# Transposed scores issued ahead of new scores inside each slot, on TensorE

## The chip, the cores and the metric

The kernel runs on one core of a Trainium2 chip. The metric is the device time of one execution in microseconds (us). Lower is better.

## The reference

Eight sequences of 512 tokens with 128 channels go through two layers.

- Layer 0: LayerNorm, then latent attention (16 heads of 8 channels, rotary embedding, causal mask) and, from the same normalised input, a mixture of 8 experts (128 to 512 to 128, ReLU, the two best gates of a softmax). Both are added to the input.
- Layer 1: LayerNorm, then attention with 16 heads of 8 whose scores are multiplied by a sigmoid gate, mixed 0.3 to 0.7 with a second attention of 4 heads of 32, mixed again 0.85 to 0.15 with a third of 4 heads of 32 that reads the mix, and an output projection; beside it a feed-forward net (128 to 512, SiLU gate, two 512 to 512 layers with exact GELU, back to 128). Both are added to the input.

Each attention is softmax(q k^T * scale) v over 512 keys. The GELU layers are evaluated once per sequence each.

## The kernel before

**Units.** All attention work is cut into groups: per sequence four of kind `a0` (layer 0, 4 heads of 8 each), four of kind `a1` (layer 1), one `ca` and one `mc` (4 heads of 32 each). A group has 8 units. Unit j works on query (or key) block c = j // 2 of 128 rows and on two heads, those of pair j % 2. So there are 80 groups and 640 units.

**Slots.** The program is one long list of slots, numbered G. Every engine walks the same list and issues in each slot what is due there. `UNIT[G]` is the unit whose scores are made in slot G, `TRANS[G]` the unit whose transposed scores are made there; it is the unit of slot G - 15 (`LAG`). A sequence takes 80 slots; in the steady part the score units fill them without a gap, in the order `a0` x4 (slots 0 to 31 of the 80), `ca` (32 to 39), `a1` x3 (40 to 63), `mc` (64 to 71), `a1` (72 to 79). In the text "slot 52" means slot 52 of a sequence's 80. Only the last sequence is laid out differently.

**What a unit does.** `score` issues two matmuls, scores of 128 queries against the keys, into banks 0 and 1. Before each it waits until VectorE has taken the row maximum of the tile that was in that bank (`pe.wait_ge(sem("max"), tile - 1)`). `reduce_unit` on VectorE (L714, and L710 with the causal mask for `a0`) takes that maximum of each. Ten slots later the maxima of a group are transposed (`max_rows`), written out by VectorE (`mrow`, L721) and sent by DMA into an extra row of the queries. 15 slots later `trans` issues the two transposed matmuls (keys against queries, with the maximum already subtracted) into banks 2 and 3; before each it waits until ScalarE has taken the exponential of the tile that was there (`sem("exp")`). `exp_unit` on ScalarE (L981) makes the probabilities. Every second slot `value` multiplies them with the values into bank 4 (8 matmuls, or 4 and 4 that sum the probabilities).

**Shapes on TensorE.** Units of `a0` and `a1` use 32 rows of the array for one head: pair 0 uses rows 0 to 63, pair 1 rows 64 to 127. In the profile their scores are `banks<-kp,qs` (32*128) and their transposed scores `banks<-qs,kp` (32*128). Units of `ca` and `mc` use 96 rows for the scores and 97 for the transposed ones, both shown as `banks<-qkc`, once as 96*128 and once as 97*128. As the lag is odd and all groups of the steady part start at even slots, score and transposed score of a slot always belong to opposite pairs there.

**The order inside a slot.** TensorE's loop is written out by hand: `score`, `trans`, `few_rows` (small projections), `value`, `few_cols` (with `max_rows`), `experts`, `ffn`, `heads`, `opening`, `between`, `mixing`, `ffn`. VectorE's is: first FFN steps, `reduce_unit`, then heads, experts, normalisations, casts (`gelu1_hi`, `gelu2_hi`, L885) and divisions. ScalarE's is: `gelu`, a copy, `exp_unit`, then experts (`hm` L1041, `h_hi` L1042), FFN, projections. All waits are semaphore counts; they name the producer's count and not a slot, so the order of TensorE's list can be altered without altering another engine's list.

**Where GELU stands.** ScalarE makes the GELU of 128x2048 at the start of slot 71 (first layer) and of slot 6 of the following 80 (second layer), with a load of its function table before (L1076) and one back for the exponential (L981).

Of the kernel before, what the change touches and what calls it, by code (L numbers as in the profile page):

```python
# [202 lines left out]
def build(nc, x_in, wide_in, lat_in, cols_in, rows_in, const_in, split_in, am_in, cons_in, b2_in, out):  # L203
# [10 lines left out]
    TRANS = {at + LAG: unit for at, unit in UNIT.items()}  # L214
# [25 lines left out]
    with ctx:  # L240
# [99 lines left out]
        def sem(name):  # L340
            if name not in sems:
                sems[name] = ctx.enter_context(nc.semaphore(name))
            return sems[name]
# [13 lines left out]
        def mm(bank, cols_, lhsT, rhs, start, stop, rows_=slice(0, P)):  # L357
            return nc.tensor.matmul(psum[rows_, bank, cols_], lhsT, rhs, start=start, stop=stop)  # L358
# [10 lines left out]
        def ch(c):  # L369
            return slice(c * P, (c + 1) * P)  # L370

        def main(g):
            return g.main >= 0

        def width(g, c):
            return (P * (c + 1), P * c) if g.kind == "a0" else (T, 0)
# [7 lines left out]
        with nc.Block() as block:  # L384

            @block.tensor
            def _(pe):
# [9 lines left out]
                def score(g, j):  # L397
                    c, pair = j // 2, j % 2
                    kw, _ = width(g, c)
                    if j == 0:  # L400
                        if main(g):
                            pe.wait_ge(sem(f"kq{g.gr}"), 32 * (g.main // NG + 1))
                        else:
                            pe.wait_ge(sem("qkc"), 96 * (g.mix + 1))
                    for s in range(2):
                        h, tile = 2 * pair + s, 2 * (8 * g.n + j) + s
                        if tile >= 2:
                            pe.wait_ge(sem("max"), tile - 1)
                        if main(g):
                            lhsT, rhs = qs[32 * h:32 * h + 32, g.gr, ch(c)], kp[32 * h:32 * h + 32, g.gr, 0:kw]  # L410
                        else:
                            lhsT, rhs = qc[0:96, h, ch(c)], kc[0:96, h, 0:kw]
                        mm(SCO + s, slice(0, kw), lhsT, rhs, True, True).then_inc(sem("score"), 1)
# [8 lines left out]
                def trans(g, j):  # L422
                    c, pair = j // 2, j % 2
                    _, q0 = width(g, c)
                    if j == 0:
                        pe.wait_ge(sem(f"qmax{g.n % 2}"), QMAX[g.n])
                    for s in range(2):
                        h, tile = 2 * pair + s, 2 * (8 * g.n + j) + s
                        if tile >= 2:
                            pe.wait_ge(sem("exp"), tile - 1)  # L430
                        if main(g):
                            lhsT, rhs = kp[32 * h:32 * h + 32, g.gr, ch(c)], qs[32 * h:32 * h + 32, g.gr, q0:T]
                        else:
                            lhsT, rhs = kc[0:97, h, ch(c)], qc[0:97, h, q0:T]
                        mm(TRA + s, slice(q0, T), lhsT, rhs, True, True).then_inc(sem("trans"), 1)
# [59 lines left out]
                def few_rows(G):  # L495
                    for k, name in enumerate(("k0", "k0r")):
                        if (b := due(G, name)) is not None:
                            taken(pe, "u", "latT", b)
                            own("n", name, b)
                            project(N, latw[:, 128 * k:128 * k + 128], latT[:, :]).then_inc(sem("n_full"), 1)  # L500
                    if (b := due(G, "v0a")) is not None:
                        own("m", "v0a", b)
                        for c in range(NC):
                            last = mm(M, slice(P * c, P * c + 96), latT[:, ch(c)], latw[:, 256:352], True, True)
                        last.then_inc(sem("m_full"), 1)
                    if (b := due(G, "v0b")) is not None:
                        own("m", "v0b", b)
                        for c in range(NC):
                            last = mm(M, slice(32 * c, 32 * c + 32), latT[:, ch(c)], latw[:, 352:384], True, True)
                        last.then_inc(sem("m_full"), 1)  # L510
                    if (b := due(G, "wo0")) is not None:
                        if b == 0:
                            pe.wait_ge(sem("b2_in"), NC * 16)
                        taken(pe, "m", "gT", b)
                        own("m", "wo0", b)
                        mm(M, slice(0, T), gT[:, :], b2[:, :], True, False)

                def few_cols(G):
                    if (u := UNIT.get(G - 10)) is not None and u[1] == 0:
                        max_rows(u[0])  # L520
                    if (b := due(G, "latT")) is not None:
                        own("u", "latT", b)
                        taken(pe, "u", "lat", b)
                        for c in range(NC):
                            last = nc.tensor.transpose(psum[0:LAT, U, ch(c)], latn[:, c, :], C("ident"))
                        last.then_inc(sem("u_full"), 1)
                    if (b := due(G, "gT")) is not None:
                        pe.wait_ge(sem("gates"), b + 1)
                        own("m", "gT", b)
                        nc.tensor.transpose(psum[0:NC * E, M, 0:P], gates[:, :, :].rearrange("p c e -> p (c e)"), C("ident")) \  # L530
                            .then_inc(sem("m_full"), 1)
# [137 lines left out]
                for G in range(FIRST_G, LAST_G):  # L669
                    if G == SETUP:  # L670
                        pe.wait_ge(sem("s_in"), 6 * 16)
                        nc.tensor.matmul(psum[:, 0, 0:1], am, cons, start=True, stop=True).then_inc(sem("s_am"), 1)
                    if G == GROUPS[0].start:
                        pe.wait_ge(sem("s_set"), 3)
                    if G in UNIT:
                        score(*UNIT[G])
                    if G in TRANS:
                        trans(*TRANS[G])
                    few_rows(G)
                    if G in VALUE_AT:  # L680
                        value(*VALUE_AT[G])
                    few_cols(G)
                    experts(G)
                    ffn(G, 0)
                    heads(G)
                    opening(G)
                    between(G)
                    mixing(G)
                    ffn(G, 1)
# [697 lines left out]
```

## Time and profile before

| what | value |
|---|---|
| median of 3 runs | 1888.39 us (1887.96 to 1888.41) |
| the profiled execution's own time | 1886.58 us |
| its span, first to last instruction | 1883.7 us |
| mean granted TensorE clock | 0.947 |
| TensorE matmul busy | 1682.3 us (89%) |
| VectorE / ScalarE / GpSimd busy | 1201.5 / 1172.5 / 691.6 us |
| DMA, share of 16 engines | 11.2% on the largest queue |

A busy row counts the time in which at least one instruction of that engine ran. PE is TensorE's matmuls, PEld its weight loads, which run beside matmuls; DVE is VectorE, ACT ScalarE, POOL GpSimd. A wait is the idle time of an engine before an instruction and the instruction whose end released it. Idle time of PEld is not idle time of PE: an earlier matmul may still run.

### The profile page before, as it was taken

What the parts mean: (1) busy time and instruction counts of PE and PEld (TensorE: products, weight loads), DVE (VectorE), ACT (ScalarE), POOL (GpSimd) and SP (SyncE); (2) the same over time, 40 slices, a digit from 0 to 9 for tenths busy, and PEclk for the clock granted to TensorE, in tenths of its full rate; (3) what the DMA queues carried; (4) which work ended last, traced back from release to release, by engine and by line L of the source; (5) the groups of instructions that cost most, each with busy time, mean ns of one, the idle gap of its engine ahead of it and who ended that gap; (6) DMA issues with size and microseconds to landing.
All of it is one profiled execution on the core that took longest, in us unless ns stands there. A gap on an engine that the chain in (4) does not pass through costs nothing.

```text
span 1883.7 us, 33377 instructions
## 1 busy us (share of the span) xinstructions
PE 1682.3 (89%) x12298; PEld 711.5 (38%) x12298; DVE 1201.5 (64%) x3100; ACT 1172.5 (62%) x2225; POOL 691.6 (37%) x672
## 2 busy tenths in 40 slices
PE   3886899889999999999999999999999999988976
PEld 1343453245323543245333543345333543222331
DVE  6545477556875587666866578566866577476623
ACT  2681765587556865687556865687657865645542
POOL 3463642255232642255322652255322631211120
PEclk9996999999999999999999999999999999978976
DMA  5101200110100101110100101110101100011010
GB/s 208 35 19 34 63 13 15 54 30 13 49 32 28 36 30 40 40 35 13 49 29 26 41 24 41 44 35 13 47 23 35 35 23 24 29 40 34 1 34 6
DMA packets 63682, 66.81 MB, mean 35 GB/s; under 512 B 8144, under 2 KB 58144, under 8 KB 62624
## 3 DMA queue, kind: packets, MB, share of 16 engines
q1 hardware_dynamic: 63520, 64.68, 11.2%
q8 instruction: 98, 1.61, 0.4%
q14 instruction: 64, 0.52, 0.1%
HBM read 40.73 MB, written 23.59 MB: 34 GB/s over the span
## 4 chain that ended last, share of the span: by engine, by line
PE 68%; DVE 15%; ACT 11%; issue 5%; POOL 1%; DMA 1%; SPq 0%; POOLq 0%; ACTq 0%; DVEq 0%
PE banks L358 66%; DVE negmax L714 7%; ACT probs L981 3%; ACT h_hi L1042 2%; ACT hm L1041 2%; DVE h L877 2%; DVE xs L814 1%; ACT L981 1%; ACT h L1076 1%; PE banks L573 1%; DVE mrow L721 1%; DVE h L872 1%; DVE r_b L902 1%; ACT L1076 1%; PE banks L580 0%
## 5 line engine op out<-in xcount | busy, mean ns | idle before, releaser
L981 ACT ACTIVATE probs<-banks 128x512 f32<-128x512 f32 (+3 forms) x1280 | 613.6, 533 | 475.4 <-PE banks L358 471.1
L714 DVE TENSOR_REDUCE negmax<-banks 128x1 f16<-128x512 f32 x768 | 492.0, 684 | 172.5 <-PE banks L358 169.1
L1141 POOL TENSOR_TENSOR h_lo<-hm,h_hi 128x512 f16<-128x512 f32 x256 | 296.7, 1160 | 387.1 <-ACT h_hi L1042 386.9
L710 DVE CUSTOM_DVE_ANT_0 scr<-banks,mask_row 128x384 f32<-128x384 f32 (+3 forms) x512 | 230.2, 487 | 211.9 <-PE banks L358 210.3
L358 PE MATMUL banks<-kp,qs 32*128 32x512 f16 (+3 forms) x1024 | 234.6, 363 | 51.5 <-DMA kp<-relk 22.5
L358 PE MATMUL banks<-probs,vp 128*32 128x512 f32 (+3 forms) x2048 | 247.3, 556 | 0.0
L1041 ACT ACTIVATE hm<-banks,cols 128x512 f32<-128x512 f32 x256 | 176.4, 689 | 113.6 <-PE banks L358 111.7
L358 PE MATMUL banks<-qs,kp 32*128 32x512 f16 (+3 forms) x1024 | 201.7, 358 | 35.2 <-ACT probs L981 33.0
L1182 POOL TENSOR_TENSOR h_lo<-h,h_hi 128x512 f16<-128x512 f32 x96 | 110.6, 1169 | 293.7 <-ACT h_hi L1070 218.3
L358 PE MATMUL banks<-w_hi,h_hi 128*128 128x128 f16 x1152 | 205.6, 221 | 0.0
L358 PE MATMUL banks<-w_lo,h_hi 128*128 128x128 f16 x1152 | 205.2, 220 | 0.0
L358 PE MATMUL banks<-w_hi,h_lo 128*128 128x128 f16 x1152 | 205.1, 220 | 0.0
L358 PE MATMUL banks<-qkc 97*128 97x512 f16 (+1 forms) x512 | 166.8, 399 | 13.8 <-DVE negmax L714 5.5
L358 PE MATMUL banks<-xh,w_hi 128*128 128x512 f16 x320 | 128.0, 400 | 54.5 <-ACT h_hi L1042 34.2
L1042 ACT ACTIVATE h_hi<-banks,cols 128x512 f16<-128x512 f32 x256 | 175.1, 684 | 0.0
L358 PEld LDWEIGHTS banks<-kp,qs 32*128 32x128 f16 x1024 | 61.1, 92 | 283.4 <-issue 108.2
L358 PEld LDWEIGHTS banks<-w_hi,h_hi 128*128 128x128 f16 x1152 | 113.4, 98 | 31.8 <-issue 12.5
L358 PE MATMUL banks<-xl,w_hi 128*128 128x512 f16 x320 | 124.9, 390 | 0.0
L358 PE MATMUL banks<-xh,w_lo 128*128 128x512 f16 x320 | 124.6, 389 | 0.0
L358 PEld LDWEIGHTS banks<-w_lo,h_hi 128*128 128x128 f16 x1152 | 113.5, 99 | 19.9 <-issue 0.8
L358 PEld LDWEIGHTS banks<-w_hi,h_lo 128*128 128x128 f16 x1152 | 113.5, 98 | 0.0
L1133 POOL TENSOR_TENSOR halves<-w,halves 128x512 f16<-128x512 f32 x64 | 74.2, 1159 | 99.4 <-ACT halves L1001 97.4
(149 smaller groups left out, 2347.7 us busy)
## 6 DMA issues: line engine op xcount, KB each, us to landing
qkc<-relm SPq DMA_DIRECT2D x96, 128.0 KB, 3.1
qs<-relq SPq DMA_DIRECT2D x64, 128.0 KB, 2.1
kp<-relk SPq DMA_DIRECT2D x64, 128.0 KB, 2.2
relm<-halves SPq DMA_DIRECT2D x32, 256.0 KB, 2.2
relq<-halves SPq DMA_DIRECT2D x16, 256.0 KB, 2.1
relk<-halves SPq DMA_DIRECT2D x16, 256.0 KB, 2.1
h<-split_in SPq DMA_DIRECT2D x3, 1024.0 KB, 5.1
xs<-x_in SPq DMA_DIRECT2D x8, 256.0 KB, 3.3
```

What stands on the lines that cost most here:

```text
L358: return nc.tensor.matmul(psum[rows_, bank, cols_], lhsT, rhs, start=start, stop=stop)
L573: last = nc.tensor.transpose(psum[:, M, ch(c)], osb[:, g.main % 2, ch(c)], C("ident"))
L710: v.tensor_tensor_reduce(scr[:, s, 0:kw], psum[:, SCO + s, 0:kw], mask_row[:, T - kw:T], -1.0, 3e38, ALU.add, ALU.min, negmax[:, g.n % 2, ...
L714: v.tensor_reduce(negmax[:, g.n % 2, c, h:h + 1], psum[:, SCO + s, 0:kw], AX.X, ALU.max, negate=True).then_inc(sem("max"), 1)
L877: v.tensor_scalar(h32[:, o, :], psum[:, U, :], V(f"hs{n}", o), None, ALU.mult) \
L981: a.activation(probs[:, c % 2, 2 * pair + s, q0:T], psum[:, TRA + s, q0:T], ACT.Exp, scale=SCALE[main(g)]).then_inc(sem("exp"), 1)
L1041: a.activation(hm[:, i % 2, :], psum[:, U, :], ACT.Relu, bias=V("b1", i))
L1042: a.activation(h_hi[:, (e + 1) % 2, hc, :], psum[:, U, :], ACT.Relu, bias=V("b1", i)) \
L1076: a.activation(h32[:, :, :], h32[:, :, :], ACT.Gelu).then_inc(sem("gelu"), 1)
L1133: p_.tensor_tensor(out=halves[:, w, 1, :], in0=w32[:, w, :], in1=halves[:, w, 0, :], op=ALU.subtract).then_inc(sem(f"low{w}"), 1)
L1141: p_.tensor_tensor(out=h_lo[:, (e + 1) % 2, hc, :], in0=hm[:, i % 2, :], in1=h_hi[:, (e + 1) % 2, hc, :], op=ALU.subtract).then_inc(sem("h ...
L1182: p_.tensor_tensor(out=h_lo[:, k % 2, o, :], in0=h32[:, o, :], in1=h_hi[:, k % 2, o, :], op=ALU.subtract).then_inc(sem("g_lo"), 1)
```

## The change

Two steps of TensorE's loop change places. Nothing else is edited: no instruction, wait, buffer or DMA is added or removed, and the lists of the other engines are the same.

```diff
                     if G == GROUPS[0].start:
                         pe.wait_ge(sem("s_set"), 3)
+                    if G in TRANS:
+                        trans(*TRANS[G])
                     if G in UNIT:
                         score(*UNIT[G])
-                    if G in TRANS:
-                        trans(*TRANS[G])
                     few_rows(G)
                     if G in VALUE_AT:
                         value(*VALUE_AT[G])
```

## Rows read from the trace of the kernel before

**Rows 1.** The page: busy time (share of the span), and the chain by engine.

```profile
PE 1682.3 (89%) x12298; PEld 711.5 (38%) x12298; DVE 1201.5 (64%) x3100; ACT 1172.5 (62%) x2225; POOL 691.6 (37%) x672
...
PE 68%; DVE 15%; ACT 11%; issue 5%; POOL 1%; DMA 1%; SPq 0%; POOLq 0%; ACTq 0%; DVEq 0%
```

**Rows 2.** Waits, whole span: engine line waited for: us in total, times, longest.

```profile
PEld banks L358 <- DVE negmax L714: 133.1, 249, 1.7
...
PEld banks L358 <- ACT probs L981: 68.8, 121, 3.6
...
PEld banks L358 <- DVE negmax L710: 42.4, 73, 3.0
```

**Rows 3.** Timeline of PE, slot 18: start us, us, instruction xcount.

```profile
832.69 0.28 PE L358 MATMUL banks<-kp,qs 32*128 32x256 f16 x2
832.70 0.34 PE L358 MATMUL banks<-qs,kp 32*128 32x384 f16 x2
```

**Rows 4.** Timeline of PE, slot 53.

```profile
919.49 0.39 PE L358 MATMUL banks<-kp,qs 32*128 32x512 f16 x2
919.81 0.61 PE L358 MATMUL banks<-qkc 97*128 97x512 f16 x2
```

**Rows 5.** Timeline of PE, slot 52 (brackets: idle before, and its releaser).

```profile
916.23 0.39 PE L358 MATMUL banks<-kp,qs 32*128 32x512 f16 x1
916.78 0.39 PE L358 MATMUL banks<-kp,qs 32*128 32x512 f16 x1 [0.17 <-DVE negmax L714]
917.10 0.61 PE L358 MATMUL banks<-qkc 97*128 97x512 f16 x2
917.63 0.64 PE L358 MATMUL banks<-probs,vc 128*32 128x512 f32 x4
```

**Rows 6.** Timeline of DVE and ACT, slots 51 and 52.

```profile
915.46 2.49 DVE L714 TENSOR_REDUCE negmax<-banks 128x1 f16<-128x512 f32 x4
915.55 1.08 ACT L981 ACTIVATE probs<-banks 128x512 f32<-128x512 f32 x2 [1.89 <-PE banks L358]
```

**Rows 7.** Timeline of PE, slot 79.

```profile
991.78 0.39 PE L358 MATMUL banks<-kp,qs 32*128 32x512 f16 x1
992.31 0.39 PE L358 MATMUL banks<-kp,qs 32*128 32x512 f16 x1
...
993.07 0.38 PE L358 MATMUL banks<-h_hi,w_hi 128*128 128x512 f16 x1
```

**Rows 8.** Timeline of PE, slot 38.

```profile
884.83 0.39 PE L358 MATMUL banks<-qkc 96*128 96x512 f16 x1 [0.21 <-DVE negmax L714]
```

**Rows 9.** Timeline of ACT, between the exponentials of slot 5 and the second GELU.

```profile
800.20 1.28 ACT L1076 ACT_TABLE_LOAD   x1
```

**Rows 10.** Timeline of PE, slots 664 to 667, first and last row.

```profile
1687.59 1.20 PE L358 MATMUL banks<-kp,qs 32*128 32x512 f16 x2 [0.59 <-DVE negmax L714]
...
1693.71 1.03 PE L358 MATMUL banks<-qkc 97*128 97x512 f16 x2
```

**Rows 11.** Timeline of PE, slots 7 and 8, behind the second GELU.

```profile
803.75 0.39 PE L358 MATMUL banks<-kp,qs 32*128 32x512 f16 x2
805.46 0.78 PE L358 MATMUL banks<-qs,kp 32*128 32x512 f16 x2 [1.33 <-ACT probs L981]
...
806.93 0.23 PE L358 MATMUL banks<-kp,qs 32*128 32x128 f16 x2
```

**Rows 12.** Timeline of DVE, slot 7.

```profile
804.17 0.69 DVE L710 CUSTOM_DVE_ANT_0 scr<-banks,mask_row 128x512 f32<-128x512 f32 x1 [0.88 <-PE banks L358]
```

**Rows 13.** Timeline of PE, slots 42 and 43.

```profile
893.99 0.71 PE L358 MATMUL banks<-qs,kp 32*128 32x384 f16 x2
...
895.84 0.39 PE L358 MATMUL banks<-kp,qs 32*128 32x512 f16 x2
```

**Rows 14.** Timeline of PE, slot 72, behind the first GELU; slot 73 starts at 977.98.

```profile
975.09 1.08 PE L358 MATMUL banks<-qs,kp 32*128 32x512 f16 x2 [2.27 <-ACT probs L981]
...
977.98 0.61 PE L358 MATMUL banks<-kp,qs 32*128 32x512 f16 x2
```

## The prediction

> **What bounds the kernel now.** I read the page first: matmuls are busy for 89% of the span, and the chain that ended last runs through TensorE for 68%, VectorE for 15% and ScalarE for 11% [rows 1]. So time is won or lost where TensorE stands still or where its list is held up. The waits over the span say by whom: the weight loads stood before maxima of VectorE for 133.1 + 42.4 = 175.5 us in 322 places, and before exponentials of ScalarE for 68.8 us in 121 [rows 2]. The first are waits of `score`, the second of `trans`. These are the two waits whose order the change swaps, and none of these sums is a gain as it stands: much of it lies beside matmuls that still run. The timelines of single slots tell what each is worth. One steady sequence repeats the last to a few hundredths, so a slot read once stands for its six or seven siblings.
>
> **Two kinds of slot.** In 48 of 80 slots both units use 32 rows a head, on opposite halves of the array. All four matmuls then run at once: scores at 832.69, transposed scores at 832.70, 0.34 us for all [rows 3]. Without a wait, either order costs the same, and with one the pair that waits still takes the other beside it. In the other 32 slots (0 to 6, 32 to 39, 47 to 54, 64 to 71, 79) one of the two fills the array, and they follow each other: transposed scores start 0.32 us behind the scores [rows 4], and two full ones take 0.44 (917.10 to 917.63 less the 0.09 of a change of tile form) [rows 5]. There the one in front can fill a wait of the other.
>
> **What the change brings, part by part.** Instructions: the same ones, 2560 score and transposed-score matmuls, no DMA moved. SP's and POOL's lists are untouched; their waits are on counts that still come.
>
> *Slot 52 and its like.* The slot's first score starts at 916.23, the second waits for its maximum until 916.78, and 0.32 and 0.53 us go by behind it before the next step at 917.63 [rows 5]. With the full transposed scores in front, they run during that wait: the exponentials they need end at 915.55 + 1.08 = 916.63 [rows 6], and 0.3 earlier once slot 51 also has its transposed scores in front. The second score then goes at about 917.04, since slot 51's scores, 0.53 later there, start their reduction at 915.69 and not 915.46 [rows 6]. The next step comes 0.31 behind, at 917.35: gain 0.3 us, seven times, 2.0 us. Slot 79 is the clean case: 0.53 us between the scores (991.78, 992.31), the next step at 993.07 [rows 7]; with the transposed scores done in the wait it comes at 992.31 + 0.32 = 992.63: gain 0.44, six times, 2.6 us. Slot 38 waits 0.21 us at its second score [rows 8]; I take 0.15, seven times, 1.0 us. In slots 34 and 48 the maxima are late because the scores before them were just in time; these move later with the swap, and I count nothing.
>
> *Ahead of the second GELU.* The table load starts as slot 5's exponentials end [rows 9], and slot 5's transposed scores come 0.3 us sooner. The GELU's input is due almost when the load ends, so I take 0.2, six times, 1.2 us. Between 0 (input later) and 0.3.
>
> *Slots 664 to 667,* in the last sequence, hold nothing but scores and full transposed scores and take 6.1 us from 1687.59 to 1693.71 [rows 10]. VectorE needs 4 x 1.25 = 5.0 us for their maxima [rows 6]: gain 1.0.
>
> Gains together: 2.0 + 2.6 + 1.0 + 1.2 + 1.0 = 7.8 us.
>
> *What is put behind a late exponential.* In slot 7 the scores go at 803.75 and the transposed scores, held by GELU and table load, at 805.46 and, 0.78 less one matmul of 0.39 later, 805.85; slot 8 starts at 806.93 [rows 11]. VectorE now uses the stall: it reduces from 804.17 (0.42 behind the score) to 805.5 [rows 12]. With the swap the scores stand behind the transposed ones and go at 805.85, their second maximum is there at 805.85 + 0.42 + 1.3 = 807.6, and slot 8's second score waits for it, 0.6 to 0.7 us after the slot's start. Queued behind it: slot 8's probabilities times values, then slots 9 and 10, each of which hands ScalarE its next tile, so little of it is absorbed. Slot 8's transposed scores are already out in front, so I take 0.56 of 0.65; five times, plus 0.3 for the first, where VectorE is late in any case: 3.1 us. VectorE's casts of the GELU's output behind these reductions move 2.1 us later too, as does GpSimd's work on them; the matmuls that read it come slots later, so I count nothing.
>
> *Slot 42* is the same in small: transposed scores at 893.99 and, 0.71 less one matmul of 0.34 later, 894.36, for exponentials that are late, and slot 43 at 895.84 [rows 3, 13]. The scores move to 894.36, their second maximum to 894.36 + 0.42 + 1.3 = 896.1, and slot 43's second score waits 0.25 to 0.3 for it: seven times, 2.1 us.
>
> *Slot 72*, behind the first GELU, has the longest stall, 2.27 us before 975.09 [rows 14], but slot 73 starts only at 977.98. The scores would go at 975.6 and their maxima be done at 975.6 + 0.42 + 1.3 = 977.3: in time. Cost 0; if the two casts behind it delayed slot 73's maxima, 0.4 each.
>
> Losses together: 5.2 us. **Sum:** -7.8 + 5.2 = -2.6, say -3 us.
>
> **Two rules of the Trainium skill.** Rows 5 show that nothing of TensorE's list passes a waiting matmul: the transposed scores, whose exponentials were ready at 916.63, start 0.32 behind the score that waited until 916.78. The Trainium skill says the same (TensorE: Matmul & The Clock Gate, Part 3: Packing small matmuls): matmuls start and end in program order. It speaks against the change: by it all 5.2 us of losses stand, whereas if scores could pass the held transposed ones the sum would be -7.8. The other rule (TensorEngine Tiling (Array Packing), Key Properties) is that a change of tiling form drains the array. The rows bear it out with 0.31 to 0.32 from one form to the next against 0.22 within one. The new order saves one change in eight value slots of a sequence (full transposed scores next to full work) and adds one in eight (full scores between 32-row and column-tiled ones): net 0; the added ones alone would be 64 x 0.09 = 5.8 us.
>
> **The rivals.**
> *B, faster: the waits for maxima are simply covered.* For it: they outweigh the waits for exponentials, 175.5 to 68.8 us [rows 2], and transposed scores in front also feed ScalarE earlier, which idles before them. Against it: most of them stand in slots where all four matmuls run at once. Slots 38, 52 and 79 wait 0.21, 0.55 and 0.53 us [rows 5, 7, 8], 1.3 a sequence; with slots 34 and 48 at half of the larger ones each it is an estimated 1.8. If all of it goes (1.8 x 7 = 12.6 us) and the losses are absorbed: 1876 us.
> *C, slower: VectorE is fed late.* Place: the slots behind a late exponential and the 32 slots of unlike shapes, where scores come 0.32 to 0.53 later. It decides from the point where the next slot starts less than 0.42 + 1.3 = 1.7 us behind the late score. Then the gains of slots 38, 52 and the GELU vanish as the maxima move along, slot 7 costs its full 0.65 and slot 72 its 0.4. Price: 6 x 0.65 + 2.1 + 8 x 0.4 = 9.2, less slot 79's 2.6: +6.6, or 1895 us. For it: VectorE idles before these reductions only because it gets them early, and slot 7 shows it clearly. Against it: most slots are over 2 us.
> *D, no effect:* the two steps are exchangeable, as rows 3 have it for 48 of 80 slots: 1888 +- 1.
>
> **How the numbers follow.** The profiled execution took 1886.58 us, 2.9 more than its span of 1883.7, and the median is another 1.8 above, 1888.39. I lay -2.7 on the median: 1885.7. Chances: forecast 0.42 (own range -6 to +1, about 1882 to 1889), B 0.27, C 0.24, D 0.07. A measurement of this kernel tells about 0.2%, 3.8 us. Faster by more: B's 0.27 and 0.12 of the forecast, 0.39. Slower by more: 0.22 of C and 0.02, 0.24. Within: 0.37. The range reaches to B's and C's prices, 1877 to 1896.
>
> **What would show it.** Right: in slots 52 and 79 the next step comes 0.3 and 0.44 us sooner; in slot 8 the second score starts about 0.6 behind the first; waits for maxima sum to less than 175.5 and those for exponentials to more than 68.8; slots of rows 3 look as before with the names exchanged. Wrong: a loss behind slot 72, a changed stretch 56 to 62 (VectorE's own pace there, where I count nothing), or four matmuls that no longer run at once.

## The result, and the profile after

The changed kernel takes 1903.59 us (median; 1903.01 to 1906.62) against 1888.40 us for the kernel before in the same comparison: ratio 1.008, 95% interval [1.0063, 1.0098], so 15.2 us slower. I had forecast 2.7 us faster, with a range to 1896: the sign was wrong and the time lies outside the range. The profiled execution took 1903.01 us, with a span of 1901.3 against 1883.7.

The page of the changed kernel, busy time and chain, as in [rows 1]:

```profile
PE 1692.0 (89%) x12298; PEld 715.1 (38%) x12298; DVE 1214.9 (64%) x3100; ACT 1170.6 (62%) x2225; POOL 694.8 (37%) x672
...
PE 69%; DVE 12%; ACT 10%; issue 5%; POOL 3%; DMA 1%; SPq 0%; POOLq 0%; ACTq 0%; DVEq 0%
```

Its waits over the span, as in [rows 2]:

```profile
PEld banks L358 <- ACT probs L981: 145.8, 236, 4.1
...
PEld banks L358 <- DVE negmax L714: 59.8, 149, 1.4
...
PEld banks L358 <- DVE negmax L710: 32.8, 52, 3.0
```

Waits for maxima fell from 175.5 to 92.6 us, waits for exponentials rose from 68.8 to 145.8. The change does to the waits what it should; their sum even falls by 6 us while the kernel gets 15 us slower. VectorE has 13.4 us more busy time for the same 3100 instructions, and POOL enters the chain with 3% instead of 1%.

TensorE in the changed kernel, slot 52, as in [rows 5] (start us, us, instruction xcount):

```profile
927.14 0.62 PE L358 MATMUL banks<-qkc 97*128 97x512 f16 x2
927.69 0.74 PE L358 MATMUL banks<-kp,qs 32*128 32x512 f16 x2
928.37 1.06 PE L358 MATMUL banks<-probs,vc 128*32 128x512 f32 x8
```

The next step comes 1.23 us behind the slot's start; it was 1.40. And slot 79, as in [rows 7]:

```profile
788.12 0.60 PE L358 MATMUL banks<-qkc 97*128 97x512 f16 x2
788.66 0.39 PE L358 MATMUL banks<-kp,qs 32*128 32x512 f16 x2
788.98 0.39 PE L358 MATMUL banks<-h_hi,w_hi 128*128 128x512 f16 x1
```

0.86 us to the next step, before 1.29: a gain of 0.43 for the 0.44 predicted. So the gains are there. Three places show how the losses arise; all three are steps that VectorE does late.

**Behind the second GELU.** TensorE in the changed kernel, slots 8 to 10, as in [rows 11]; slot 8 starts at 814.72:

```profile
815.46 0.22 PE L358 MATMUL banks<-kp,qs 32*128 32x128 f16 x1 [0.23 <-DVE negmax L710]
...
818.14 0.43 PE L358 MATMUL banks<-kp,qs 32*128 32x128 f16 x2 [0.28 <-DVE negmax L710]
...
819.86 1.93 PE L358 MATMUL banks<-probs,vp 128*32 128x512 f32 x8
```

and the same last step in the kernel before:

```profile
811.19 1.06 PE L358 MATMUL banks<-probs,vp 128*32 128x512 f32 x8
```

Slot 8's second score comes 0.74 us behind the slot's start (I had 0.6 to 0.7). What I had not: the scores of slots 9 and 10 wait for maxima as well, so that from slot 8's start to that last step 5.14 us go by and not 4.26. Then the eight matmuls take 1.93 us and not 1.06: the granted clock is 0.52 from 819.80 to 823.00, close to the lower of its two levels (1.2 of 2.4 GHz). That fall is not the swap's alone; in two other sequences the kernel before has one in these slots too (see the first experiment). Why slots 9 and 10 wait is seen on VectorE. The kernel before:

```profile
805.89 1.08 DVE L885 CAST h_hi<-h 128x512 f16<-128x512 f32 x3
807.20 0.29 DVE L710 CUSTOM_DVE_ANT_0 scr<-banks,mask_row 128x128 f32<-128x128 f32 x1 [0.22 <-PE banks L358]
```

The changed kernel:

```profile
815.82 2.06 DVE L885 CAST h_hi<-h 128x512 f16<-128x512 f32 x3
817.79 0.28 DVE L710 CUSTOM_DVE_ANT_0 scr<-banks,mask_row 128x128 f32<-128x128 f32 x1
```

and beside it, on GpSimd of the changed kernel:

```profile
816.16 1.43 POOL L1141 TENSOR_TENSOR h_lo<-hm,h_hi 128x512 f16<-128x512 f32 x1 [21.13 <-ACT h_hi L1042]
```

The casts stand behind slot 7's late maxima and in front of slot 8's. Pushed back, they meet a GpSimd subtraction that before started at 808.38, when they were over; the third of them takes 1.39 us where each took 0.42 before.

**Slot 687**, behind the first GELU of the last sequence. The kernel before, TensorE and then VectorE:

```profile
1754.69 1.09 PE L358 MATMUL banks<-qs,kp 32*128 32x512 f16 x2 [2.53 <-ACT probs L981]
1755.71 2.08 PE L358 MATMUL banks<-wide,ctxT 128*128 128x128 f32 x8
```

```profile
1752.20 1.29 DVE L714 TENSOR_REDUCE negmax<-banks 128x1 f16<-128x512 f32 x2 [0.49 <-PE banks L358]
...
1753.68 0.29 DVE L828 TENSOR_TENSOR onorm<-banks,rden 128x128 f32<-128x128 f32 x1
```

The changed kernel, TensorE and then VectorE:

```profile
1766.97 0.87 PE L358 MATMUL banks<-qs,kp 32*128 32x512 f16 x2 [2.63 <-ACT probs L981]
1767.47 0.60 PE L358 MATMUL banks<-kp,qs 32*128 32x512 f16 x2
1769.75 1.65 PE L358 MATMUL banks<-wide,ctxT 128*128 128x128 f32 x6 [1.69 <-DVE onorm L828]
```

```profile
1767.92 1.29 DVE L714 TENSOR_REDUCE negmax<-banks 128x1 f16<-128x512 f32 x2 [3.71 <-PE banks L358]
...
1769.41 0.29 DVE L828 TENSOR_TENSOR onorm<-banks,rden 128x128 f32<-128x128 f32 x1
```

TensorE stands 1.69 us for a division whose inputs were long there. It stood on VectorE's list behind maxima of scores that now sit on TensorE's list behind exponentials. So a wait of TensorE on ScalarE holds up VectorE's unrelated work, and that comes back to TensorE.

**Slot 34,** one of the slots that my prediction counted as nothing, shows the same without any late exponential. A step of TensorE waits there for the one in which VectorE writes `vc`, behind slot 33's maxima; slot 33's scores come later with the swap, as it is a slot of unlike shapes. The kernel before, then the changed kernel:

```profile
874.77 0.38 PE L358 MATMUL banks<-ident,negmax 128*4 128x128 f16 x4 [0.20 <-DVE vc L852]
```

```profile
885.54 0.38 PE L358 MATMUL banks<-ident,negmax 128*4 128x128 f16 x4 [0.46 <-DVE vc L852]
```

### The profile page after: what moved, and what is told of

It is laid out like the page before. It is cut to its first block, busy times and chain, and to the rows that moved or that the text cites. A ratio compares the mean times of both kernels' runs of the same rounds, so it can differ in the third digit from the quotient of the medians.

```text
span 1901.3 us, 33377 instructions
## 1 busy us (share of the span) xinstructions
PE 1692.0 (89%) x12298; PEld 715.1 (38%) x12298; DVE 1214.9 (64%) x3100; ACT 1170.6 (62%) x2225; POOL 694.8 (37%) x672
## 4 chain that ended last, share of the span: by engine, by line
PE 69%; DVE 12%; ACT 10%; issue 5%; POOL 3%; DMA 1%; SPq 0%; POOLq 0%; ACTq 0%; DVEq 0%
PE banks L358 67%; DVE negmax L714 5%; ACT probs L981 3%; ACT h_hi L1042 2%; ACT hm L1041 2%; POOL h_lo L1141 1%; DVE xs L814 1%; PE banks L573 1%; ACT L981 1%; DVE h L877 1%; DVE r_b L902 1%; ACT h L1076 1%; DVE h L872 1%; POOL xs L1186 0%; DVE mrow L721 0%
## 5 line engine op out<-in xcount | busy, mean ns | idle before, releaser
L358 PE MATMUL banks<-kp,qs 32*128 32x512 f16 (+3 forms) x1024 | 227.5, 366 | 41.6 <-DMA kp<-relk 22.3
L358 PE MATMUL banks<-qs,kp 32*128 32x512 f16 (+3 forms) x1024 | 210.4, 359 | 49.6 <-ACT probs L981 44.8
L358 PE MATMUL banks<-probs,vp 128*32 128x512 f32 (+3 forms) x2048 | 252.2, 566 | 0.0
L358 PEld LDWEIGHTS banks<-qs,kp 32*128 32x128 f16 x1024 | 55.2, 91 | 249.7 <-ACT probs L981 117.1
```

## The experiments

Theories, as the expectations name them: **L**, lateness: a score put behind a late exponential gives VectorE its maxima late, and its work and the next slots are late with it. **Q**, the part of L that is VectorE's queue: steps that need nothing of the late score wait behind its maxima. **K**, clock: more of the stretches fall to the lower granted clock. **V**, the diffuse part of L: VectorE gets its scores 0.3 to 0.5 us later in every slot of unlike shapes. (One expectation calls the clock theory C.) Each time stands beside that of the kernel before in the same comparison, and a difference "by ratio" is the ratio times that time. Most kernels differ in one condition alone, written here as the slots in which the transposed scores go first:

```diff
+ ahead = G in TRANS and (CONDITION)
+ if ahead:
+     trans(*TRANS[G])
  if G in UNIT:
      score(*UNIT[G])
- if G in TRANS:
+ if G in TRANS and not ahead:
      trans(*TRANS[G])
```

**Where the loss is.** Behind the second GELU:

```diff
+ CONDITION: 80 <= G < 640 and 7 <= G % 80 <= 11
```

> The swapped order only in slots 7 to 11 of each steady sequence (behind the second GELU), the old order in all others. Theory L (the loss is local: scores put behind late exponentials, there and in the first and last sequence): the trace of the full swap is longer than before by 6.6 us in total in slots 6 to 12 of these sequences, so about +6.5 us over the kernel before. Theory V (diffuse: VectorE gets its scores 0.3 to 0.5 us later in the 32 unlike slots of every sequence): at most +1.5 us.

Measured: 1894.40 against 1888.33 us, ratio 1.0019 [1.0004, 1.0033]. Single executions lie in two groups, 1884.6 to 1889.6 and 1892.7 to 1896.9, so a size can't be read from it to better than +0.8 to +6 us. The traces are sharper. Slots 6 to 11 of one sequence, in the kernel before at the full clock, in the kernel before where the clock falls, and with the swap at the full clock (window, length, busy time of each engine, granted clock, DMA share, GB/s):

```profile
1226.80:1243.00 16.20, 13.54 (x110) 5.05 (x109) 11.46 (x39) 14.66 (x22) 6.79 (x6) 1.00 0.01 2
```

```profile
1012.90:1030.70 17.80, 15.06 (x106) 5.14 (x105) 11.46 (x39) 14.74 (x22) 6.78 (x6) 0.90 0.00 1
```

```profile
1226.50:1243.60 17.10, 13.74 (x107) 5.22 (x107) 12.54 (x39) 14.70 (x22) 7.40 (x6) 1.00 0.01 2
```

From slot start to slot start that is 16.21, 17.85 and 17.10 us: 0.9 us a sequence for the swap, and 1.6 us for a fall of the clock without the swap (1.0 to 1.6 with it). It falls in two of five such sequences in the trace of the kernel before, in four in that of the changed kernel, and in one in this run's, whose profiled execution (1884.62 us) is of the lower group. That the number of such falls makes the two groups is not shown.

The first sequence alone:

```diff
+ CONDITION: G < 80
```

> The swapped order only in the first sequence (slots 17 to 79 from the start of the list), the old order from slot 80 on. Theory L: the full swap's trace has gained 4.2 us by slot 80, from slots 24 to 31, where VectorE is late with the weight splits and TensorE then shows a granted clock of 0.5; so +4 us, and it stays to the end. Theory V: the unlike slots are hardly there in this stretch, so about 0.

Measured: 1889.11 us, 1.0006 [0.9998, 1.0015]: nothing that can be told from no change; the 4 us that L expected are not there.

The last sequence alone:

```diff
+ CONDITION: G >= 640
```

> The swapped order only in the last sequence, from slot 640. Theory L: +4 us (the full swap's trace loses 6.6 us in slots 685 to 695, behind the last GELU, and gives back 3.6 in slots 662 to 673 and 706 to 710). Theory V: +2 us, spread over the stretch.

Measured: 1897.79 us, 1.0049 [1.0037, 1.0061], +9.3 us by ratio: a large part of the whole, from 38 of the 584 slots that hold both steps, and twice what L expected.

The slots of unlike shapes, in the steady sequences:

```diff
+ CONDITION: 80 <= G < 640 and (G % 80 < 7 or 32 <= G % 80 < 40 or 47 <= G % 80 < 55 or 64 <= G % 80 < 72 or G % 80 == 79)
```

> The swapped order only in the 32 unlike slots of each steady sequence (0 to 6, 32 to 39, 47 to 54, 64 to 71, 79), the old one elsewhere. Theory L: -2 to 0 us, since the gains of slots 52 and 79 are here and no late exponential is. Theory V: +5 to +9 us, most of the loss.

Measured: 1891.36 us, 1.0007 [0.9991, 1.0022]: nothing that can be told from no change, and under the +5 of theory V.

The slots in which all four matmuls run at once, without those behind the second GELU:

```diff
+ CONDITION: 80 <= G < 640 and (12 <= G % 80 < 32 or 40 <= G % 80 < 47 or 55 <= G % 80 < 64 or 72 <= G % 80 < 79)
```

> The swapped order only in the like slots of each steady sequence except 7 to 11 (12 to 31, 40 to 46, 55 to 63, 72 to 78). Theory L: the only late exponentials here are those of slots 42 and 72; the full swap's trace has 0.37 us more per sequence around slot 42 and 0.2 to 0.7 around slot 72, so +3 to +6 us. Theory C (the granted clock: what the swap costs is mostly more time at 0.5 behind longer idle stretches): no sum from single slots, a spread of runs of 5 us and more.

Measured: 1902.59 against 1888.00 us, 1.0079 [1.0066, 1.0092], +14.9 us by ratio. This was the surprise: slots in which "either order costs the same" make as much loss as the whole change. No trace shows it in full: the profiled execution took 1895.32 us, the other four 1902.36 to 1903.42, and its swapped stretches are 0.74 us a sequence longer at the same clock, some 5 us together. Its granted clock falls in slots 6 to 11 of four sequences, and those slots have the old order here.

The slots that my prediction had as gains, alone:

```diff
+ CONDITION: 80 <= G < 640 and G % 80 in (5, 38, 52, 79) or 664 <= G <= 667
```

> The swapped order only where the prediction counted gains: slots 5, 38, 52 and 79 of each steady sequence and slots 664 to 667. If those terms were right: -7.8 us. By the full swap's trace, which is 0.54 us shorter a sequence around slot 79, 0.31 around slot 5 and at most 0.36 around slot 52: -1.2 x 7 = -8 us at best. If the gains there came from whole stretches of swapped slots and not from these: about 0.

Measured: 1881.38 us, 0.9969 [0.9958, 0.9980], -6.6 us between the medians (-5.9 by ratio) for a predicted -7.8.

**What makes the last sequence slow.** All its slots swapped, and VectorE makes slot 687's division before it turns to the slot's maxima:

```diff
+ CONDITION: G >= 640
+ if G == 687: heads(G)
  if G in UNIT: reduce_unit(*UNIT[G])
+ if G != 687: heads(G)
- heads(G)
```

> The swapped order in the last sequence only, as in e3_last_seq (+9 us), and in slot 687 alone VectorE's division of the attention output (heads) goes ahead of its two reductions. Theory Q (queue: in slot 687 TensorE's next step waits 1.69 us for that division, which stands behind reductions that came 3.4 us late): 1.8 us of the loss go, and with them what the clock at 0.5 makes of them, 3 to 4 us; so +5 us over the kernel before. If the loss is the late scores as such, it stays at +9.

Measured: 1890.96 us, 1.0014 [1.0004, 1.0024]: from +9.3 to about +2.6 us. TensorE of this kernel in slot 687:

```profile
1758.81 0.87 PE L358 MATMUL banks<-qs,kp 32*128 32x512 f16 x2 [2.63 <-ACT probs L987]
...
1759.82 1.44 PE L358 MATMUL banks<-wide,ctxT 128*128 128x128 f32 x8
```

The wait of 1.69 us is gone while TensorE's order and its wait for the exponentials are unchanged. That shows the queue on VectorE as the cause of that wait and of most of the last sequence's loss. Slot 687 swapped alone:

```diff
+ CONDITION: G == 687
```

> The swapped order in one slot only, 687, behind the last GELU. Theory Q: the whole of the 1.8 us and the clock's share, +2 to +5 us from one slot of 640. A theory by which many slots of the last sequence share its loss: under +1 us.

Measured: 1891.03 us, 1.0020 [1.0012, 1.0029], +3.8 us by ratio from one slot of 584. That is less than the 6.7 us that VectorE's order in this slot gave back above; why, no run tells.

**What makes the like slots slow.** Three pieces of them. First, slot 72 alone, where my prediction had 0:

```diff
+ CONDITION: 80 <= G < 640 and G % 80 == 72
```

> Transposed scores in front only in slot 72 of the steady sequences, 7 slots in all (behind the first GELU, whose exponentials are the latest of a sequence). The step where my prediction had cost 0. Theory L (VectorE's work order: the late scores hand VectorE its maxima late, and casts and slots 73 to 76 stand behind them): in the trace with all like slots swapped, stretch 70 to 76 is 0.45 us longer a sequence, so +3 us, about 1891. Theory K (clock: a stretch behind the idle time falls to the lower granted clock in more sequences, at 1.5 to 2 us each): +5 to +10, 1893 to 1898, with spread between executions. Prediction's step: 0, 1888.

Measured: 1895.09 against 1889.47 us, 1.0035 [1.0023, 1.0047], +6.6 us by ratio (4.3 to 8.9), from 7 slots. Two more pieces:

```diff
+ CONDITION: 80 <= G < 640 and (12 <= G % 80 < 32 or 55 <= G % 80 < 64)
```

> Transposed scores in front only in slots 12 to 31 and 55 to 63 of the steady sequences: both units use 32 rows a head there, nearly no exponential is late, and the stretches have the same length to 0.01 us in all traces. Theory L: no effect, 1888 within 1 us. Theory K (granted clock falls more often by small shifts of order): +2 to +8. If the sum of the like slots (+14.6 us) sits here, neither GELU nor slot 42 is the cause.

Measured: 1892.84 us, 1.0021 [1.0012, 1.0030], +4.0 us by ratio. Its trace has all swapped stretches as long as before to 0.1 us and is longer only in the first and last sequences, which it doesn't change. Not explained.

```diff
+ CONDITION: 80 <= G < 640 and 40 <= G % 80 < 47
```

> Transposed scores in front only in slots 40 to 46 of the steady sequences; slot 42 has late exponentials. My prediction's term: +2.1 us. Trace with all like slots swapped: stretch 33 to 45 is 0.34 us longer, 45 to 55 is 0.22 shorter: +0.8 to +2.4, so 1889 to 1891. Theory K: as that, and clock on top, over 1892.

Measured: 1891.30 us, 1.0013 [1.0004, 1.0022], +2.5 us by ratio (predicted for slot 42: +2.1). In its trace slots 40 to 44 are 0.37 us longer a sequence and slots 45 to 54 0.23 shorter, which leaves 1.0 us. The three pieces sum to 13.1 of the 14.9 us; slots 73 to 78 were not measured alone.

**Clock or queue.** Eight matmuls whose results are overwritten (the filler) put into TensorE's idle time ahead of slots 72 and 687, in the kernel before and in the changed one:

```diff
+ if 80 <= G < 640 and G % 80 == 72 or G == 687:
+     pe.wait_ge(sem("max"), 2 * 8 * UNIT[G][0].n + 2 * UNIT[G][1])
+     for k in range(8):
+         mm(SCO + k % 2, slice(0, T), w_hi[:, 0:P], w_hi[:, 0:T], True, True)
```

> The order of before, and 8 added matmuls of 128 columns (results overwritten, about 2 us) ahead of the two steps of slot 72 of the steady sequences and of slot 687, where TensorE stands idle for the GELU. The scores of these slots go some 1.8 us later, the transposed ones are not held longer. Theory L (late scores cost, as with the swap): +3 to +6 us, 1891 to 1894. Theory K (idle time in front of the heavy stretch lowers the granted clock behind it): the filler takes part of the idle time away, low clock in slots 72 to 80 becomes less than the 4.5 us a sequence of before and the time falls by 5 to 10 us, or the two cancel.

Measured (order of before): 1885.16 against 1889.47 us, 0.9985 [0.9970, 1.0001]: not told from no change, where L expected +3 to +6. Its trace is 4.4 us shorter than that of the kernel before in the steady sequences and 4.6 longer from slot 640 on, where slot 687's scores come late.

> The changed kernel (all slots swapped) with the 8 overwritten matmuls in front of slot 72 of the steady sequences and slot 687, where its transposed scores wait 2.6 to 2.9 us for the exponentials behind the GELU. Theory K (idle time ahead of these stretches lowers the clock behind them, which is part of the +15.2 us): 1890 to 1898. Theory L (the loss is lateness of scores and of VectorE's work): no change, 1903 +- 2, as the filler lies in the wait and feeds nobody.

Measured (changed kernel): 1900.25 us, 1.0063 [1.0048, 1.0077]; the changed kernel itself has 1.0080 [1.0063, 1.0098]. The two intervals overlap, so the medians don't tell whether the filler helped; its profiled execution is the slowest of its six, 1908.48 us. The windows of slots 70 to 75 of one sequence tell more, first the order of before with the filler, then the swapped order with it:

```profile
758.20:776.40 18.20, 16.01 (x83) 5.01 (x81) 12.44 (x21) 12.71 (x19) 6.87 (x7) 1.00 0.06 16
```

```profile
765.30:784.10 18.80, 16.70 (x83) 5.26 (x82) 12.26 (x20) 12.22 (x18) 6.80 (x7) 1.00 0.06 16
```

| granted clock in slots 70 to 75 | order of before | swapped |
|---|---|---|
| 1.00 (with the filler) | 18.18 us | 18.83 us |
| 0.91 | 18.32 | 18.84 |
| 0.82 | 18.86 | 19.04 |

At full clock throughout the swap costs 0.65 us, more than at the lower ones (0.10 of it belongs to slot 70). So keeping the clock up does not take the loss away, and K fails for this stretch.

How far does a shift without a cause move the time? Two overwritten matmuls, in slot 16 of the first sequence:

```diff
+ if G == 16: two of the added matmuls
```

> The order of before; two added matmuls of 128 columns (overwritten) ahead of the two steps of slot 16 of the first sequence, where TensorE stands idle for 2 us anyway. No theory has work for it: the added instructions shift the rest by at most 0.4 us. If small shifts alone move where the granted clock falls, the median differs from before by 2 to 4 us in either direction; if not, by less than 1. That sets what the effects of +1 to +4 us of the other experiments may be called.

Measured: 1889.68 against 1888.86 us, 1.0009 [0.9997, 1.0020]. Its one profiled span is 1893.0, 9.3 us over that of the kernel before, for 0.8 us between the medians. A part of that is luck of the one trace of the kernel before: up to slot 80 it took 169.4 us, and the 14 other kernels that change nothing up to there 172.1 to 174.9. Two single traces may differ by that much. What may be compared is a stretch that repeats over the sequences, at the same granted clock: slots 22 to 32 took 28.39 us in six of the seven steady sequences, in this kernel and in the kernel before.

**The queue behind slot 72 removed.** Slot 72 swapped as above, and VectorE casts the GELU's output before it turns to slot 72's maxima:

```diff
+ CONDITION: 80 <= G < 640 and G % 80 == 72
+ early = 80 <= G < 640 and G % 80 == 72
+ if early: ffn(G)
  if G in UNIT: reduce_unit(*UNIT[G])
  ...
+ if not early: ffn(G)
- ffn(G)
```

> As the run with transposed scores in front in slot 72 alone (+6.6 us), but VectorE casts the output of the first GELU before it turns to slot 72's late scores, not behind them. In that run VectorE stood idle 3.9 us before the reduction and then had reductions and casts in one queue, the two casts beside GpSimd at 1.20 and not 0.75. Theory L (the loss is that queue): most of it comes back, +0 to +3, 1889 to 1892. Theory K (the loss is the granted clock in slots 6 to 12 and 72 to 76): it stays at +5 to +7, 1894 to 1896.

Measured: 1890.04 against 1888.50 us, 1.0008 [0.9996, 1.0019]: of +6.6 us some 5 come back, though TensorE waits as long for its exponentials (2.89 us in both). VectorE in slots 72 to 74 of one sequence, first the kernel before, where slot 73 starts at 977.98:

```profile
972.56 1.29 DVE L714 TENSOR_REDUCE negmax<-banks 128x1 f16<-128x512 f32 x2 [0.18 <-PE banks L358]
973.77 0.75 DVE L885 CAST h_hi<-h 128x512 f16<-128x512 f32 x2
978.62 1.29 DVE L714 TENSOR_REDUCE negmax<-banks 128x1 f16<-128x512 f32 x2 [4.10 <-PE banks L358]
979.82 1.12 DVE L885 CAST h_hi<-h 128x512 f16<-128x512 f32 x2
```

then slot 72 swapped, where slot 73 starts at 984.88:

```profile
983.09 1.29 DVE L717 TENSOR_REDUCE negmax<-banks 128x1 f16<-128x512 f32 x2 [3.91 <-PE banks L358]
984.30 1.20 DVE L888 CAST h_hi<-h 128x512 f16<-128x512 f32 x2
985.52 1.29 DVE L717 TENSOR_REDUCE negmax<-banks 128x1 f16<-128x512 f32 x2
986.73 1.51 DVE L888 CAST h_hi<-h 128x512 f16<-128x512 f32 x2
988.16 1.28 DVE L717 TENSOR_REDUCE negmax<-banks 128x1 f16<-128x512 f32 x2
```

and with the casts first, where slot 73 starts at 981.28:

```profile
976.35 0.76 DVE L888 CAST h_hi<-h 128x512 f16<-128x512 f32 x2 [0.78 <-ACT h L1086]
979.49 1.29 DVE L717 TENSOR_REDUCE negmax<-banks 128x1 f16<-128x512 f32 x2 [2.37 <-PE banks L358]
981.92 1.29 DVE L717 TENSOR_REDUCE negmax<-banks 128x1 f16<-128x512 f32 x2 [1.14 <-PE banks L358]
983.12 1.01 DVE L888 CAST h_hi<-h 128x512 f16<-128x512 f32 x2
```

In the kernel before the reduction of slot 72 and two casts lie in TensorE's stall. Swapped, VectorE idles through it (3.91 us) and then has no idle time from 983.09 on, with slower casts. With the casts first, the idle time is back (1.14 us). TensorE meets this in slot 75. Its first score in the kernel before (both scores in one row), with slot 72 swapped, and with the casts first; the second score waits 0.21 us in both of the latter:

```profile
982.94 0.39 PE L358 MATMUL banks<-kp,qs 32*128 32x512 f16 x2
```

```profile
988.90 0.38 PE L358 MATMUL banks<-kp,qs 32*128 32x512 f16 x1 [0.44 <-DVE negmax L717]
```

```profile
984.79 0.39 PE L358 MATMUL banks<-kp,qs 32*128 32x512 f16 x1
```

And the windows of slots 70 to 75 in another sequence, at the same granted clock, in the same order:

```profile
755.20:773.50 18.30, 15.53 (x75) 4.54 (x73) 11.48 (x21) 12.93 (x19) 6.65 (x7) 0.91 0.05 16
```

```profile
761.50:780.30 18.80, 15.08 (x75) 4.42 (x73) 12.32 (x20) 12.91 (x19) 6.79 (x7) 0.91 0.06 16
```

```profile
758.40:776.70 18.30, 14.99 (x75) 4.50 (x73) 11.37 (x21) 12.93 (x19) 6.65 (x7) 0.91 0.06 16
```

The 0.5 us that the swap costs there are gone with VectorE's order alone. Over seven sequences they would make 3.5 of the 6.6 us.

The rest may lie in the clock, which is not shown. In one of the seven sequences, the trace with slot 72 swapped took 18.3 us for slots 6 to 11, at a granted clock of 0.63; the kernel before and the one with the casts first took 16.0 us for the same order there, at 0.79. But the stretch varies without a cause too: the kernel with two added matmuls took 16.46 us for it, at 0.79. Here the clock does cost, and which executions it hits isn't settled.

**The same mending for the whole change**: all slots swapped, the casts ahead of the maxima in slots 7 and 72, the division ahead of them in slot 687:

```diff
+ CONDITION: True
+ early = 80 <= G < 640 and G % 80 in (7, 72)
+ if early: ffn(G)
+ if G == 687: heads(G)
  if G in UNIT: reduce_unit(*UNIT[G])
  ...
+ if G != 687: heads(G)
- heads(G)
  ...
+ if not early: ffn(G)
- ffn(G)
```

> The changed kernel (all slots swapped) with VectorE's list following it at the three places behind the GELU: casts ahead of the maxima in slots 7 and 72 of the steady sequences, the head sums ahead of the maxima in slot 687. Theory L: slot 72 gives back up to 6, slot 7 up to 3, slot 687 up to 7 of the +15.2: 1889 to 1894. Theory K: 1900 to 1904, as the idle time of TensorE in front of these slots is not touched.

Measured: 1896.62 us, 1.0040 [1.0025, 1.0056], +7.6 against +15.2 us, less back than L's 1889 to 1894. So VectorE's order at three places is about half of the loss. (The profiled execution, 1889.81 us, is the fastest of nine.)

**A version faster than both.** Slots whose maxima are late and whose exponentials are not:

```diff
+ CONDITION: 80 <= G < 640 and G % 80 in (0, 1, 2, 3, 4, 5, 38, 52, 79) or 664 <= G <= 667
```

> Transposed scores in front where they fill the array next to a wait for maxima and no exponential is late: slots 0 to 5, 38, 52 and 79 of the steady sequences and 664 to 667. The gain slots gave -6.6 us; slots 0 to 4 start their next slot 0.05 to 0.2 us sooner in the traces with them in front (0.35 a sequence, 7 sequences: -2.4 us). Expected 1879 to 1880; if slots 0 to 4 add nothing, 1881.5.

Measured: 1877.99 against 1888.86 us, 0.9945 [0.9931, 0.9959], 10.4 us faster. And with the eight added matmuls in slot 72:

```diff
+ if 80 <= G < 640 and G % 80 == 72: the eight added matmuls
```

> The same slots in front, and the 8 overwritten matmuls ahead of the two steps of slot 72 of the steady sequences alone. The filler lowered slow-clock time in slots 72 to 76 from 4.5 to 0.5 us a sequence and the time by 2.8 us; in slot 687, now without filler, it had cost: 4.6 us more in the last sequence of that trace. If both hold and add up: 1874 to 1877. If the filler was luck of the clock: 1879 to 1882.

Measured: 1877.49 us, 0.9939 [0.9922, 0.9956]: the same. In its trace less of the span is at the lower clock (mean granted clock 0.956 against 0.947), for nothing that the medians show.

**What the traces add up to.** The steady sequences repeat so closely that the changed kernel can be laid beside the kernel before stretch by stretch, from slot start to slot start, both at the same granted clock (1.00, but 0.91 in slots 70 to 75). Us in one sequence; the last column is what my prediction had for the stretch:

| slots | before | changed | VectorE's order mended | changed less before | predicted |
|---|---|---|---|---|---|
| 0 to 5 | 17.56 | 17.14 | 17.14 | -0.42 | 0 |
| 6 to 11 | 16.21 | 17.04 | 16.60 | +0.83 | +0.36 |
| 12 to 21 | 26.11 | 26.08 | 26.08 | -0.03 | 0 |
| 22 to 39 | 47.49 | 47.92 | 47.92 | +0.43 | -0.15 |
| 40 to 54 | 34.65 | 34.67 | 34.66 | +0.02 | 0 |
| 55 to 62 | 21.10 | 21.16 | 21.16 | +0.06 | 0 |
| 63 to 69 | 19.96 | 20.37 | 20.37 | +0.41 | 0 |
| 70 to 75 | 18.31 | 18.84 | 18.54 | +0.53 | 0 |
| 76 to 79 | 9.36 | 8.90 | 8.90 | -0.46 | -0.44 |
| sum | 210.75 | 212.12 | 211.37 | +1.37 | -0.23 |

The first of the eight sequences has no scores in slots 32 to 79 and the second none in 64 to 71, so sequences 2 and 3 lack some of these swaps (it is not only the last that is laid out differently). With that the stretches make about 8 us over the seven steady sequences. From slot 640 to the end the changed kernel took 256.3 us, where the ten kernels that change nothing there took 248.9 to 254.7, half of them 251.6 or less: about 5 us more. The first sequence shows no difference (173.6 to slot 80, against the 172.1 to 174.9 above). That is some 13 of the 15.2 us, by an estimate from single traces; the rest is within what the clock's falls do.

## Why the prediction was wrong

- **Gains, -7.8 us: right in the main.** The gain slots alone gave -6.6, and their traces have slot 52 at 0.31 us (predicted 0.3), slot 38 at 0.16 (0.15), the GELU at 0.16 (0.2) and slot 79 at 0.35 (0.44). Slots 664 to 667 gained 0.8 us for 1.0: from slot 663's scores to the step behind slot 667, 8.88 us before and 8.11 with the swap. In the changed kernel slot 52 gained only 0.17, as its scores are late there themselves. Slots 0 to 4 gained 0.4 that I hadn't counted.
- **Slot 7, +3.1 us: mechanism right, size too small.** Slot 8's wait was as predicted. The failed sentence is "VectorE's casts ... move 2.1 us later too, as does GpSimd's work on them; ... so I count nothing". The cost of the casts is not who reads them but who stands behind them: slot 8's maxima, 1.0 us later for the casts' 2.06 instead of 1.08 us, and slots 9 and 10 wait. It is 0.9 us a sequence at the full clock for my 0.56, and 0.44 of it comes back with the casts in front.
- **Slot 42, +2.1 us: right** within the measurement (+2.5 for slots 40 to 46), though its trace shows a part coming back by slot 54.
- **Slot 72, "Cost 0": the step that failed most clearly**, +6.6 us measured alone. I asked when the *next* slot needs the late maxima (977.3, in time for 977.98) and that answer was right: slot 73 doesn't wait. I didn't ask what else of VectorE the stall had been carrying. One reduction and two casts had lain in it and were pushed into slots 73 to 75, which fill VectorE, and slot 75 waits. Casts first gives some 5 of the 6.6 back. My hedge, 0.4 a sequence, named the casts and was near what the traces show (0.5); the rest of the 6.6 is in no trace.
- **Slots 34, 36 and 63 to 70: counted as nothing.** Of slots 34 and 48 I wrote that their maxima "move later with the swap, and I count nothing". Slot 34 takes 0.38 us more, and slots 22 to 39 together 0.43 where I had -0.15. Slots 64, 66, 68 and 70 take 0.10 more each, and slots 0 and 2 0.10 less. That has the size and the places of my term for the change of tile form (0.09), whose net 0 stands; but in slots 63 to 69 it is a loss of 0.41.
- **Slot 687: left out.** I argued from the steady sequences and let "seven times" stand for the rest. The last sequence, where the list is laid out otherwise, gave +9.3 alone, of which VectorE's order in one slot is about 7.
- **"Either order costs the same" [rows 3]: true of the slot, not of its place.** It holds where nobody is late: slots 12 to 21 and 55 to 62 are as long as before to 0.06 us. The slots behind both GELUs are like slots too.
- **Rival C, slower, 1895 us,** had the right owner, VectorE fed late, and both places, with the wrong test: "the point where the next slot starts less than 0.42 + 1.3 = 1.7 us behind the late score". Slot 73 starts later than that, and slot 72 was among the costliest of all.
- **Range:** it ended at C's price, and had no room for terms I had set to 0. The clock had no term at all, though a fall in slots 6 to 11 costs 1.0 to 1.6 us in either order. (The text has the sum as -2.6, -3 and -2.7 in three places; the forecast uses the last.)

What stays open: the medians of the parts don't add up. Behind the second GELU, first and last sequence, unlike and like slots sum to 3.6 + 1.1 + 9.3 + 1.3 + 14.9 = 30 us by ratio, the whole is 15.2. The traces do nearly add up, at the same clock, so what is counted twice or comes on top is most likely in the clock's falls; no run shows that. The like slots' median is the plainest case: +14.9 us, of which its trace has some 5. The +4.0 us of slots 12 to 31 and 55 to 63 have no place in a trace. Of the mended change's +7.6 us the table has 0.62 a sequence, in slots 6 to 11, 22 to 39, 63 to 69 and 70 to 75; these were not mended one by one.

## What to carry to other kernels

When a step is moved behind a late wait, list what its consumer's engine does during that wait, not only when the result is needed: the stall of one engine is often the slack of another. Engines that work through a list in order need their orders changed together: unrelated work (casts, divisions) belongs ahead of the step that now comes late. And swap only where it pays: nine slots of eighty and four of the last sequence gave -10 us, all of them +15. And before two traces are compared, put stretches of the same granted clock side by side: one fall of the clock in slots 6 to 11 cost up to 1.6 us here, the swap of slot 72 0.5 us a sequence.

## What the runs showed of the hardware

- A cast of 128x512 f32 to f16 on VectorE took 0.42 us alone and 1.39 beside a GpSimd subtraction of 1.43 us on the same kind of tiles; three in a row 1.08 and 2.06. The Trainium skill (SBUF — State Buffer, Who interferes with whom) has the cause as a lock: such a cast can use a pair of ports that VectorE shares with GpSimd, and who comes second waits for the whole instruction. The trace agrees: the long cast started 0.33 us behind the subtraction and ended 0.29 us behind its end. It is a price of moving work in time that no count of instructions shows.
- Nothing on VectorE passed a reduction that waited for its score. The Trainium skill (PSUM — Partial Sum Buffer, Engine vs sequencer instructions) says that the queues of ScalarE, VectorE and GpSimd are strictly first in, first out. The trace agrees: VectorE stood idle for 3.91 us, and for the last 3.2 of them the GELU's output that the casts behind needed was done.
- The granted clock fell to 0.63 in one stretch of one kernel and was 0.79 in the same stretch of another with the same work in the same order; slots 6 to 11 took 16.2 us at 1.00 and 17.8 at 0.90, again with the same work in the same order. In slots 70 to 75 it mattered far less: 0.01 us between 1.00 and 0.91 in the swapped order, 0.14 in the old one. The mean granted clock says little before it is known whether TensorE sets the pace there.
